# Key rows packed in halves and quarters of tiles, and the low halves of the weighted dots subtracted on GpSimd

## The reference, cut to what matters

```python
dots = jnp.einsum('hqnd,hqmd->hqnm', f_q, f_k)
cosine_sim = dots / (qn[..., :, None] * kn[..., None, :])
var_component = jnp.einsum('hqn,hqm->hqnm', q_ratio, k_ratio)
mixed = cw * cosine_sim + vw * cov_component + ww * var_component
out = jnp.einsum('hqnm,hqmd->hqnd', mixed, f_v)     # f_k and f_v are the same projection of the 77 keys
out = out.transpose(1, 2, 0, 3).reshape(q.shape[0], q.shape[1], H * D)
return out @ w_out.T + b_out
```

## Time and profile before

| what | value |
|---|---|
| median of 3 runs | 1376.34 us (1375.95 to 1377.22) |
| the profiled execution's own time | 1375.92 us |
| its span | 1373.3 us |
| mean granted TensorE clock | 0.977 |
| PE busy | 1268.7 us, 92% |
| DVE busy | 1117.0 us, 81% |
| ACT busy | 1027.6 us, 75% |
| GpSimd busy | 191.5 us, 14% |

### The profile page before, as it was taken

How to read it: one execution, slowest core, us unless ns; L and a number is a source line. 1 busy time by engine, 2 the same in 40 slices (tenths; PEclk the granted TensorE clock), 3 DMA queues, 4 the chain that set the end, 5 groups by cost and what they waited for, 6 DMA issues and landing times.

```text
span 1373.3 us, 34972 instructions
## 1 busy us (share of the span) xinstructions
PE 1268.7 (92%) x10770; PEld 797.6 (58%) x10770; DVE 1117.0 (81%) x3164; ACT 1027.6 (75%) x3398; POOL 191.5 (14%) x130
## 2 busy tenths in 40 slices
PE   4999887999999999999999999999999999999864
PEld 2667565656656565656575656565656565665521
DVE  6986665897979797979797979798989889797853
ACT  5666232687878787979696979787888878787876
POOL 2352120102020202020101101010101020202000
PEclk9999899999999999999999999999999999999976
DMA  8440011606151424242424233342415050605140
GB/s 252 140 151 19 12 33 41 199 11 193 29 176 45 161 61 153 68 153 69 153 69 141 80 122 99 100 122 78 144 59 162 31 185 6 202 19 173 35 154 16
DMA packets 163127, 141.25 MB, mean 103 GB/s; under 512 B 9326, under 2 KB 150799, under 8 KB 163088
## 3 DMA queue, kind: packets, MB, share of 16 engines
q1 hardware_dynamic: 163088, 140.76, 32.9%
HBM read 87.00 MB, written 42.55 MB: 94 GB/s over the span
## 4 chain that ended last, share of the span: by engine, by line
PE 59%; DVE 13%; issue 11%; ACT 2%; DMA 1%; SPq 1%; POOL 1%; DVEq 0%; POOLq 0%; ACTq 0%; PEldq 0%
PE work L893 17%; PE work L895 15%; PE work L894 15%; PE attended L1391 7%; PE score L1380 4%; DVE nm L1672 2%; PE work L1283 2%; DVE Vpl L1569 2%; DVE l2s L1641 1%; DVE Gl L1581 1%; DMA sqE<-sq_rows 1%; ACT prob L1479 1%; DVE x2S L1635 1%; DVE qst L1594 1%; SPq L1220 1%
## 5 line engine op out<-in xcount | busy, mean ns | idle before, releaser
L1479 ACT ACTIVATE prob<-score,nm 128x256 f32<-128x256 f32 x1024 | 470.9, 479 | 25.6 <-DVE nm L1672 19.3
L1672 DVE TENSOR_REDUCE nm<-score 128x2 f32<-128x512 f32 x512 | 337.1, 680 | 14.1 <-PE score L1380 13.3
L1479 ACT ACTIVATION_READ_ACCUMULATOR prob<-score,nm 128x1 f32 x1024 | 218.3, 213 | 0.0
L1594 DVE BATCH_NORM_STATS2 qst<-work 128x6 f32<-128x128 f32 x512 | 113.6, 283 | 102.9 <-PE work L895 102.9
L1391 PE MATMUL attended<-prob,vsp 128*32 128x256 f32 x2048 | 138.6, 395 | 14.2 <-DVE vsp L1687 11.9
L1380 PE MATMUL score<-qstack,kstack 64*128 64x256 f16 x1024 | 102.3, 279 | 17.2 <-ACT prob L1479 16.3
L893 PE MATMUL work<-woutTh,fvph 128*128 128x256 f16 x384 | 105.4, 274 | 5.6 <-DVE Vpl L1569 4.6
L1526 POOL TENSOR_TENSOR rq<-qft,mhalf 128x32 f32<-128x32 f32 x16 | 86.8, 5426 | 164.6 <-DVEq L1601 164.6
L894 PE MATMUL work<-woutTl,fvph 128*128 128x256 f16 x384 | 104.7, 273 | 0.0
L895 PE MATMUL work<-woutTh,fvpl 128*128 128x256 f16 x384 | 104.7, 273 | 0.0
L893 PE MATMUL work<-wTh,xTh 128*128 128x512 f16 x256 | 97.9, 382 | 1.9 <-DVE fvpl L1581 1.9
(11 more groups left out here) (327 smaller groups left out, 3272.4 us busy)
## 6 DMA issues: line engine op xcount, KB each, us to landing
qstack<-parts SPq DMA_DIRECT2D x64, 256.0 KB, 3.8
kstack<-parts SPq DMA_DIRECT2D x64, 256.0 KB, 4.2
sqE<-sq_rows SPq DMA_DIRECT2D x64, 154.0 KB
s_xin<-in_x SPq DMA_DIRECT2D x8, 1024.0 KB, 6.1
xin<-in_x SPq DMA_DIRECT2D x16, 512.0 KB, 3.7
x2S<-in_x SPq DMA_DIRECT2D x16, 512.0 KB, 8.0
parts<-qh SPq DMA_DIRECT2D x32, 256.0 KB, 2.4
parts<-ql SPq DMA_DIRECT2D x32, 256.0 KB, 2.5
```

Of the source, the lines that this page charges most:

```text
L1479: nc.scalar.activation(prob[:, g % PG, e, j + jj, :], sc[n % SC][:, jj * NQ:(jj + 1) * NQ], ACT.Exp, bias=nm[:, u + jj:u + jj + 1], accum_ ...
L1594: last = nc.vector.bn_stats(qst[:, t, 4 * half + h, :], bank(e)[:, h * DH:(h + 1) * DH])
L1672: nc.vector.tensor_reduce(nm[:, u:u + 2], sc[n % SC][:, :].rearrange("p (u q) -> p u q", q=NQ), AX.X, ALU.max, negate=True).then_inc(max_r ...
```

## The change

Keys are no longer packed in one row of 616. Each of the first four tiles holds the first or last 64 keys of two heads, one in the lower and one in the upper half of the tile; the fifth holds the 13 keys that each head has left, in groups of 32 rows for two heads (zeros in the gaps). So `V` and `d` are issued as matmuls of 64 columns in pairs (tiles 0 to 3) and of 32 columns in fours (tile 4), each on its own columns of the array and its own rows of the bank. `G` becomes eight steps of two heads. The few extra rows of `y` move to tiles of their own, `mE` and `vE`, which add one matmul for each half of a `y` step; ACT writes `mE` itself, twice, and the two `wq` transfers go. `sqE` is loaded by five transfers instead of twelve. The factor `MS` is put into `sqT`, so the low half of `m` is a plain subtraction, and that moves from DVE to GpSimd. `ORDER` is a new list.

```diff
-PAD = 127 + MK
-PADW = 2 * H * PAD + 127
+LEFT = MK - 64
+FS, GS = 96, 80
+LO_ROW, LL_ROW = 32, 64
+Y_ROWS = LL_ROW + H + 1
...
-rk V0 qs1 V1 V0.h V0.l S0 qpow V1.h G0 M0 G1 G0.h V1.l S1 X0 M1 G2 G1.h G0.l X1 G1.l a1 M2 G2.h S2 a1.h V2 G2.l X2
+rk S0 M0 G0 V0 M1 X0 qs1 S1 V1 V0.h X1 G0.h M2 V1.h qpow G0.l X2 V0.l a1 S2 V1.l a1.h G1 M3 G2 G1.h a1.l X3 G1.l G4 M4
...
+def value_block(h, b2):
+
+    return FS * (2 * h + b2) + LEFT * (h % 2)
+
+
+def left_block(h, b2):
+
+    return FS * (2 * h + b2) + (64 if h % 2 == 0 else -16)
...
+    def key_tile(t, b2):
+
+        if t == HT - 1:
+            return [(32 * j, 32, GS * (4 * j + 2 * b2) + 64) for j in range(H // 2)]
+        return [(64 * odd, 64, GS * (4 * t + 2 * b2 + odd) + LEFT * odd) for odd in range(2)]
...
                     for n, t in enumerate(tiles):
-                        heads = tile_heads(t)
-                        for h in heads:
-                            last = products(nc, bk[:, n * DIM:(n + 1) * DIM],
-                                            fvp, (ALL, slice(window(t, h, b2), window(t, h, b2) + P)),
-                                            w["woutT"], (ALL, h), h == heads[0], h == heads[-1])
+                        cols = slice(n * DIM, (n + 1) * DIM)
+                        if t < HT - 1:
+                            for m, (x, y) in enumerate(("hh", "hl", "lh")):
+                                for h in (2 * t, 2 * t + 1):
+                                    at = value_block(h, b2)
+                                    last = nc.tensor.matmul(bk[64 * (h % 2):64 * (h % 2) + 64, cols], fvp[x][:, at:at + 64],
+                                                            w["woutT"][y][:, h, :], start=m == 0, stop=m == 2)
+                            continue
+                        for odd in range(2):
+                            for m, (x, y) in enumerate(("hh", "hl", "lh")):
+                                for j in range(H // 2):
+                                    at = left_block(2 * j + odd, b2)
+                                    last = nc.tensor.matmul(bk[32 * j:32 * j + 32, cols], fvp[x][:, at:at + 32],
+                                                            w["woutT"][y][:, 2 * j + odd, :], start=odd == 0 and m == 0,
+                                                            stop=odd == 1 and m == 2)
...
                     for n, t in enumerate(tiles):
-                        r = HM_ROWS[t]
                         for k in range(KT):
-                            last = products(nc, bk[0:r, n * 2 * P:(n + 1) * 2 * P],
-                                            G, (ALL, k, slice(b2 * HM + t * P, b2 * HM + t * P + r)),
-                                            xT, (ALL, k, slice(b2 * NQ, (b2 + 1) * NQ)), k == 0, k == KT - 1)
+                            for m, (x, y) in enumerate(("hh", "hl", "lh")):
+                                for row, size, at in key_tile(t, b2):
+                                    last = nc.tensor.matmul(bk[row:row + size, n * 2 * P:(n + 1) * 2 * P], G[x][:, k, at:at + size],
+                                                            xT[y][:, k, b2 * NQ:(b2 + 1) * NQ], start=k == 0 and m == 0,
+                                                            stop=k == KT - 1 and m == 2)
...
+                        last = nc.tensor.matmul(bk[:, r * DIM:(r + 1) * DIM],
+                                                mE[0:Y_ROWS, c * NQ + r * P:c * NQ + (r + 1) * P], vE[0:Y_ROWS, c, :],
+                                                start=False, stop=True)
...
-                    nc.scalar.activation(wqT["h"][:], bank(e)[0:H, :], ACT.Copy, scale=MS).then_inc(hi_ready[lead(e)], 1)
...
+                    nc.scalar.activation(mE[0:H, :], bank(e)[0:H, :], ACT.Copy, scale=MS)
+                    nc.scalar.activation(mE[LL_ROW:LL_ROW + H, :], bank(e)[0:H, :], ACT.Copy, scale=MS).then_inc(hi_ready[lead(e)], 1)
...
+                elif e[0] == "m":
+                    if e.endswith(".l"):
+                        step, done = e[:-2], HALVES[lead(e)]
+                        pool.wait_ge(hi_ready[lead(e)], a * len(done) + done.index(step) + 1)
+                        dst, src, _ = emptied(step, "l")
+                        nc.gpsimd.tensor_tensor(dst, src, emptied(step, "h")[0], ALU.subtract).then_inc(m_ready, 1)
```

More of the change, by code:

```diff
@@ L41 @@
 HM_TILES = [(0, 1), (2, 3), (4,)]
-HM_ROWS = [min(P, HM - P * t) for t in range(HT)]
-KR_ROW = HM_ROWS[-1]
-ONE_ROW = KR_ROW + H
-Y_ROWS = HM_ROWS[:-1] + [ONE_ROW + 1]
 SB = NB // NG
@@ L996, in half @@
     return group, e, 2 * i, 2 * (4 * group + 2 * e + i)
-def window(t, h, b2):
-    return PAD * (2 * h + b2) + 127 + P * t - MK * h
-def tile_heads(t):
-    return [h for h in range(H) if MK * h < P * (t + 1) and MK * (h + 1) > P * t]
-SQ_LOADS = [sum(len(tile_heads(t)) for t in part) for part in ((0, 1), (2, 3, 4))]
+def value_block(h, b2):
+    return FS * (2 * h + b2) + LEFT * (h % 2)
+def left_block(h, b2):
+    return FS * (2 * h + b2) + (64 if h % 2 == 0 else -16)
+SQ_LOADS = [2, 3]
 def main_phase(nc, ctx, w, x_rows, out_rows, rk_rows, kr_rows, sq_rows, fixed_rows, parts):
@@ L1030, in main_phase @@
     rk_all, rkc = sb("rk_all", [P, HT, NB]), sb("rkc", [P, HT, 2])
-    aux, sqT, wqT = sb("aux", [P, 2, PT, H]), sb("sqT", [H, PR]), pair("wqT", [H, PR])
+    aux, sqT = sb("aux", [P, 2, PT, H]), sb("sqT", [H, PR])
     st4, qst, qft = sb("st4", [P, PT, 2]), sb("qst", [P, PT, H, 6]), sb("qft", [P, 5, PT, H])
@@ L1573, in a_part @@
                     dve.wait_ge(hi_ready[lead(e)], a * len(done) + done.index(e) + 1)
-                    drain(nc.vector.scalar_tensor_tensor(wqT["l"][:], bank(e)[0:H, :], MS, wqT["h"][:],
+                    drain(nc.vector.scalar_tensor_tensor(mE[LO_ROW:LO_ROW + H, :], bank(e)[0:H, :], MS, mE[0:H, :],
                                                          ALU.mult, ALU.subtract), e)
-                elif part == "l" and kind != "zT":
+                elif part == "l" and kind not in ("zT", "m"):
                     done = HALVES[lead(e)]
```

141 lines of the change are left out of this document (74 added, 67 removed).

## The result

The changed kernel takes **1646.59 us** (median of 4 runs, 1645.60 to 1650.50), the kernel before 1376.14 on the same chip: ratio 1.197, 95% interval [1.195, 1.200]. It is 270 us slower, where 1338 us and a gain of 38 were forecast. Times and ratios in this text are of fast runs alone: one execution of `g3_before_low_half_on_gpsimd` took 2451 us at a granted clock of 0.909 and is left out.

What follows compares the result with a forecast made beforehand. TensorE and VectorE, both nearly full in 55 us of each turn, were taken as the bound; each loses about 3 us, part returns at a1, so 16 x 2.4 = 38 us off gives 1338 us, range 1314 to 1380.

Steps and rivals of the forecast that it cites:

- the one on the transfers: sqE loads: twelve become five of about the same bytes; VectorE had waited 6.3 us; worth 0 to 6, taken as 0.
- both engines that bound the stretch lose about 3 us: In the 55 us after the turn's first 16: TensorE -2.9 us per turn, VectorE -3.15.
- the sum of -3.0 to -1.8 a turn: Whole turn: from both engines' full saving to -2.9 with 1.2 given back at a1; middle taken, -2.4 us.
- waits move to ScalarE and VectorE: Rival: the stretch shrinks only to what ScalarE allows, -0.1 to -1.6 us per turn, say 1362 us; chance 0.17.
- The stand at `a1`: Head of the turn: TensorE stands some 2.3 us until VectorE finishes G0.l, 1.07 before: +1.2 us per turn.
- Halves at 0.055 us: 64-column matmuls of V and d: pairs run side by side, 0.055 us each, the lower of two bounds.
- quarters at 0.027: 32-column matmuls of the fifth tile: four run together, 0.027 us each at the full clock.
- two rivals: Quarters held by their issue at 0.057 us, say 1370 us, chance 0.13; halves one behind the other, 1464 us, chance 0.06.
- `d` saves nothing: TensorE's d steps: 60 units of 0.1095 us per turn before and 60 after.
- its 36 units: TensorE's V steps: 72 units of 0.1095 us per turn become 36, so 36 saved.
- GpSimd at 1.16 us against 1.4: GpSimd's subtraction for m.l: 1.4 us each, six some 7 us a turn, hidden in its idle time.
- the forecast's 0.3: Sign in the profile after: no wait of VectorE's md for GpSimd's subtraction beyond 0.3 us.

Runs made afterwards that it cites:

- g3: Kernel before with the low halves of m subtracted on GpSimd, nothing else of the change: 1374.00 us, ratio 0.9985.
- h3: Kernel before with V's matmuls cut from three products to two: 1377.01 us, ratio 1.000.
- k4: Kernel before with V cut to two products and VectorE's low halves of V cut to 8 of 256 columns after the first pair: 1363.16 us.
- h1: One-row run with 24 extra matmuls a turn behind V1, into a bank that nobody waits for: 1380.50 us, ratio to before 1.004.
- g1: One-row run with the first thirty steps of the list in the old order: 1416.14 us, ratio to before 1.030.
- h2: One-row run with the drains of G0 moved ahead: 1394.35 us, ratio to before 1.012.
- h4: One-row run with the drains of G0 moved ahead and M1 put back as well: 1415.07 us, ratio to before 1.028.
- one-row run: Changed kernel with sixteen sqE loads of one source row each in place of five: 1392.1 us, ratio to before 1.013.

## Why the prediction was wrong

**The step that failed by 254 us** is the one on the transfers: "Twelve `sqE` loads become five of about the same bytes ... so this is worth 0 to 6 us; I take 0." It priced a load by its bytes and by the old wait. What counts is how many of the 16 engines carry it. Three runs fix it from both sides: one-row loads take 254 us away, the five loads put 222 into the kernel before, and 62 partitions for 64 bring 276 back. The trace of before shows no load of this form, yet the forecast put no bound on it, and none of its rivals spoke of transfers.

**The step that failed by most of the rest**, 1392 for 1338, is "both engines that bound the stretch lose about 3 us", from which the sum of -3.0 to -1.8 a turn came. The earlier trace rows give one window of 55 us for both. The two savings lie in different parts of the turn: TensorE's in `V`, two thirds of it in the first 24 us and the rest just ahead of them, and VectorE's in the dots, nearly all in the next 20. In each part the other engines, nearly as full, go on as they were. Taken one by one in the kernel before, 2.6 us a turn off TensorE in `V` are worth 0 us (h3: it waits for ScalarE and VectorE instead, and its clock falls a little), and GpSimd's part some 2 us, within the noise (g3). Where both were relieved in the same part, something came of it (k4). These runs take the savings out of the kernel before; how each of the 54 us between 1392 and 1338 came about in the changed one is shown only for the 12 of the clock. The rival "waits move to ScalarE and VectorE" had this mechanism, but with 1350 to 1374 it, too, let the savings meet.

**The head of the turn.** The stand at `a1` was forecast at 2.3 us (its own terms, 5.0 less 2.6, give 2.4) and measured at 2.77, with the right cause. What it sets off was missed: half the granted clock for the matmuls behind it, 0.7 us a turn (h1). That part is shown. How the remaining 4.7 us between h1 and before divide among ScalarE's added 0.9 us, the added drains of `G` and the list isn't: each new order of the head (g1, h2, h4) moved the waits and gained nothing.

**A slip in the sum.** Its bound of -1.8 is -3.0 with the 1.2 given back; from -2.9, as written there, it would be -1.7. This moves nothing.

**What held.** Halves at 0.055 us and quarters at 0.027, against two rivals; `d` saves nothing (6.91 us before and 7.26 in the one-row run, changes of shape and all) and `V` saves 3.7 us (8.23 before, 4.53 in h1; all summed from start to start over a turn), where its 36 units were 3.9; GpSimd at 1.16 us against 1.4; the wait at `a1` ended by `Gl`. GpSimd is hardly late: `md` waits for it 3.3 us in all in the one-row run, four times, though up to 1.7 us at a time and not the forecast's 0.3. GpSimd's part is worth 11.4 us in the changed kernel and nothing that can be told from noise in the kernel before.

Of the complete kernels tried, none beats the kernel before by more than a measurement can tell; the nearest is GpSimd's part alone, at 0.9985 [0.9969, 1.0001].
